# Transposed inputs laid out by the host, and a reordered preparation, in a two-layer cross attention

## What is computed

```
q = heads(x @ w_q);  k, v = heads(text @ w_k), heads(text @ w_v)
out = softmax(q k^T / sqrt(8)) v  +  softmax(masked or normed token scores) v_ip
x = out @ w_out + b_out + x
```

## Time and profile before

| | |
|---|---|
| median of 3 runs | 1545.47 us (1544.97 to 1546.61) |
| the profiled execution | 1546.61 us, its span 1544.8 us |
| TensorE, VectorE, ScalarE busy | 94%, 72%, 69% of the span |
| queries' block / prepare / attention starts | 0 to 38.7 / 38.7 to 200.7 / 200.7 us |

### The profile page before, as it was taken

The page is one execution under the profiler, slowest core; times in us unless marked ns, Lnnn a source line. Parts: engine busy times, 40 slices in busy tenths (PEclk is TensorE's granted clock), DMA queues, the critical chain, the costliest instruction groups (busy, mean ns, idle before and its releaser), DMA issues. The chain is left out here.

```text
span 1544.8 us, 32772 instructions
## 1 busy us (share of the span) xinstructions
PE 1456.3 (94%) x12886; PEld 911.6 (59%) x12886; DVE 1119.0 (72%) x1572; ACT 1061.7 (69%) x1962; POOL 189.6 (12%) x363
## 2 busy tenths in 40 slices
PE   6899969999999999899999999999999999999995
PEld 4455513333333333577777777777777777777774
DVE  5777778887877877876767777777777777777625
ACT  2455548877877877777777777777777777777752
POOL 4553300000101101000010000000000000000000
PEclk9899969999999999999999999999999999999996
DMA  5256741111211211100001100000011000100000
GB/s 158 67 168 196 223 101 51 51 51 51 56 47 50 64 47 47 42 23 24 20 22 34 28 20 23 26 24 23 19 26 26 23 18 25 26 23 16 7 1 18
DMA packets 82903, 75.91 MB, mean 49 GB/s; under 512 B 28608, under 2 KB 70964, under 8 KB 82756
## 3 DMA queue, kind: packets, MB, share of 16 engines
q1 hardware_dynamic: 82756, 73.88, 17.7%
HBM read 47.73 MB, written 26.09 MB: 48 GB/s over the span
## 5 line engine op out<-in xcount | busy, mean ns | idle before, releaser
L1367 DVE TENSOR_TENSOR whole<-late,whole 128x1024 f16<-128x1024 f32 (+1 forms) x280 | 320.2, 1144 | 99.7 <-ACT whole L1226 96.5
L1352 DVE TENSOR_REDUCE mx<-ps_y 128x2 f32<-128x800 f32 (+2 forms) x227 | 224.0, 987 | 106.1 <-PE ps_y L1034 105.9
L1112 PE MATMUL ps_v<-eh,whole 128*128 128x269 f16 x1040 | 292.7, 281 | 0.0
L1112 PE MATMUL ps_n<-eh,whole 128*128 128x269 f16 x1040 | 291.4, 280 | 0.0
L1226 ACT CAST whole<-late 128x1024 f16<-128x1024 f32 (+1 forms) x280 | 275.8, 985 | 8.9
L1114 PE MATMUL ps_v<-el,whole 128*128 128x269 f16 x960 | 268.9, 280 | 0.0
L1115 PE MATMUL ps_v<-eh,whole 128*128 128x269 f16 x960 | 268.8, 280 | 0.0
L1115 PE MATMUL ps_n<-eh,whole 128*128 128x269 f16 x960 | 268.1, 279 | 0.0
L1114 PE MATMUL ps_n<-el,whole 128*128 128x269 f16 x960 | 267.9, 279 | 0.0
L1352 DVE TENSOR_REDUCE mx<-ps_x 128x2 f32<-128x800 f32 (+2 forms) x198 | 195.5, 987 | 80.9 <-PE ps_x L1034 80.7
L1352 DVE TENSOR_REDUCE mx<-ps_t 128x2 f32<-128x800 f32 (+2 forms) x215 | 211.5, 984 | 32.8 <-PE ps_t L1034 32.5
(11 more groups left out here) (433 smaller groups left out, 2073.6 us busy)
## 6 DMA issues: line engine op xcount, KB each, us to landing
e<-in_ctx SPq DMA_DIRECT2D x4, 1536.0 KB
kb<-k_parts SPq DMA_DIRECT2D x80, 74.9 KB
kb<-k_parts SPq DMA_DIRECT2D x80, 74.7 KB
k_parts<-kp SPq DMA_DIRECT2D x12, 400.0 KB
vb<-v_cols SPq DMA_DIRECT2D x40, 117.0 KB, 2.0
v_cols<-late SPq DMA_DIRECT2D x4, 1040.0 KB, 10.8
late<-v_cols SPq DMA_DIRECT2D x40, 104.0 KB, 2.0
qb<-q_parts SPq DMA_DIRECT2D x160, 25.0 KB
```

Of the source, the lines that this page charges most:

```text
L1112: pe.matmul(ps, hi, eh, start=(t == 0), stop=False)
L1352: nc.vector.tensor_reduce(mx[:, pair % 2, c, :], bank("max", pair, c)[:, :, 0:w], AX.X, ALU.max).then_inc(chunk_max, 1)
L1367: nc.vector.tensor_tensor(pl[s % 2][:, t0:t0 + w, :], ring[:, turn % EXPS, 0:w], ph[s % 2][:, t0:t0 + w, :], ALU.subtract).then_inc(low_do ...
```

## The change

The host gives three more inputs: x, the context and the tokens, each transposed. The transposes and their copies in `queries` and `prepare` go. `ctxT` is loaded by DMA in four pieces for each batch (`load_piece`), a piece of the next batch when the value products no longer read its columns. The keys are sent segment by segment, each with a semaphore of its own (`k_sent[m]`); segment 0 goes out before SP waits for `el_done`. The next batch's maximum is taken behind the ninth value tile of this one, and its all-reduce follows the last third part. The second parts are cast by ScalarE. In batch 0, `scale_bits`, `high` and `low` come behind all ten key products, GpSimd's all-reduces come before its clearing, and the softmax steps move behind the values of batches 0 and 1. All loops are written out. Pairs 0 and 1 are loaded in batches 2 and 3, pairs 2 and 3 at the start of the attention. The queries' large buffers lie in `eh`. The lines of the diff that matter:

```diff
+            ctx = (ctx_in, sbuf("e32", [P, NT, C], F32, st), sbuf("ctxT", [P, 2, NPAD], F32, st),
+                   st.enter_context(nc.semaphore("ctx_loaded")), [st.enter_context(nc.semaphore(f"turned_in_{kc}")) for kc in range(4)])
+            w_ctx = (sbuf("wk", [P, 2, 2 * D], F32, st), sbuf("wv", [P, 2, 2 * D + IP[1]], F32, st), st.enter_context(nc.semaphore("weights_in")))
+            queries(nc, K, LS, banks, w, consts, QS, ctx, w_ctx, (x, bbox, spatial))
+            prepare(nc, K, L, banks, ctx, w_ctx, consts, KS, QS, VS)
...
+                def send_keys(b, m):
+                    if m < 2:
+                        sp.wait_ge(k2_done, KI * b + 4 * (m + 1))
+                        for seg, r0, rows, l, h0 in KSEG:
+                            if seg == m:
+                                for part in range(3):
+                                    dst = KS[l][h0:h0 + rows // DH, b, part]
+                                    sp.dma_start(dst, kp[r0:r0 + rows, m, part, :]).then_inc(k_sent[m], 16)
+                        return
+                    sp.wait_ge(k2_done, KI * (b + 1))
+                    for j in range(2):
+                        for part in range(3):
+                            dst = KS[1][H - KREST // DH:H, b, part].rearrange("h d (g j k) -> h d g j k", j=2, k=KC)[:, :, :, j]
+                            src = kp[KREST * j:KREST * (j + 1), 2, part, 0:2 * KC].rearrange("p (g k) -> p g k", k=KC)
+                            sp.dma_start(dst, src).then_inc(k_sent[2], 16)
+
+                def load_turned(b, kc):
+                    n = KI + min((kc + 1) * KC - 1, TOK - 1) // P
+                    if kc == 3:
+                        n = LASTF
+                    sp.wait_ge(filled[n % 8], fills(b - 1, n))
+                    load_piece(sp, consts, ctxT, turned_in, b, kc)
+
+                def send_values(b, half):
+                    t0, t1 = ((0, NT // 2), (NT // 2, NT))[half]
+                    sp.wait_ge(vh_done, NT * b + t1)
+                    sp.dma_start(VS[0][:, b, :, t0:t1].rearrange("g p t n -> p g (t n)"),
+                                 vaug[:, :, t0:t1].rearrange("p g t i n -> p g (t i n)")).then_inc(v_sent, 16)
+
+                for b in range(B):
+                    send_keys(b, 0)
+                    if b < B - 1:
+                        sp.wait_ge(el_done, 2 * (b + 1))
+                        sp.dma_start(e32[:, 0:NT - 1, :], ctx_in[b + 1, 0:P * (NT - 1)].rearrange("(t p) c -> p t c", p=P)).then_inc(ctx_loaded, 16)
+                        sp.dma_start(e32[0:LAST, NT - 1, :], ctx_in[b + 1, P * (NT - 1):TOK]).then_inc(ctx_loaded, 16)
+                    send_keys(b, 1)
...
+                        load_pair(sp, K, KS, QS, b - 2)
+                    if b < B - 1:
+                        load_turned(b + 1, 0)
+                        load_turned(b + 1, 1)
+                        send_values(b, 0)
+                        load_turned(b + 1, 2)
+                        load_turned(b + 1, 3)
+                        send_values(b, 1)
+                        sp.wait_ge(freed[LASTF % 8], fills(b, LASTF))
+                        send_cut_v(sp, K, VS, L, b)
+                sp.wait_ge(v_sent, 16 * 2 * (B - 1))
+                load_v0(sp, K, VS, 0)
+                for m in range(3):
+                    sp.wait_ge(k_sent[m], 16 * SENDS[m] * B)
...
-                turn(1)
-                with sp.Fori(2, B, 1) as b:
-                    turn(b)
-                send(B - 1)
-                sp.wait_ge(k_sent, 16 * SENDS * B)
...
-                    pe.wait_ge(ctx_loaded, 32 * (b + 1))
-                    for n in range(TR):
-                        ps = bank(n)
-                        for t in range(2 * n, min(2 * n + 2, NT)):
-                            for c in range(2):
-                                at = ((t % 2) * 2 + c) * P
-                                last = pe.transpose(ps[:, at:at + P], e32[:, t, c * P:(c + 1) * P], K["ident"][:])
-                        last.then_inc(filled[n % 8], 1)
...
+                            pe.wait_ge(turned_in[kc], 16 * (b + 1))
...
+                def second_part(b, n):
+                    m, kc = n // 4, n % 4
+                    act.wait_ge(freed[n % 8], fills(b, n))
+                    nc.scalar.copy(kp[:, m, 1, kc * KC:(kc + 1) * KC], rem[:, n % RR, :]).then_inc(k1_done, 1)
...
+                for b in range(B):
+                    for n in range(KI):
+                        m, kc = n // 4, n % 4
+                        if kc == 0 and b:
+                            act.wait_ge(k_sent[m], 16 * SENDS[m] * b)
+                        act.wait_ge(filled[n % 8], fills(b, n))
+                        nc.scalar.copy(kp[:, m, 0, kc * KC:(kc + 1) * KC], banks[n % 8][:, 0:KC]).then_inc(k0_done, 1)
+                        if n:
+                            second_part(b, n - 1)
+                        if b and n == 3:
+                            high(b)
+                    second_part(b, KI - 1)
+                    if not b:
+                        high(b)
+                    if b == 1:
...
+                def over_partitions(column, b):
+                    pool.wait_ge(amax_done, b + 1)
+                    nc.gpsimd.partition_all_reduce(amax[:, column + 1:column + 2], amax[:, column:column + 1], P,
+                                                   bass.bass_isa.ReduceOp.max).then_inc(amax_all, 1)
+
+                over_partitions(2, 0)
+                over_partitions(0, 1)
                 nc.gpsimd.memset(vaug, 0.0)
                 nc.gpsimd.memset(vcut, 0.0).then_inc(pool_init, 1)
...
+                    if b < B - 1:
+                        over_partitions(0, b + 2)
...
+                def largest(b):
+                    dve.wait_ge(ctx_loaded, 32 * (b + 1))
                     nc.vector.tensor_reduce(amax[:, 0:1], e32[:], AX.XY, ALU.max, apply_absolute_value=True).then_inc(amax_done, 1)
+
...
+                dve.wait_ge(weights_in, 64)
+                nc.vector.tensor_reduce(amax[:, 2:3], wv[:, :, D:2 * D], AX.XY, ALU.max, apply_absolute_value=True).then_inc(amax_done, 1)
+                largest(0)
+                nc.vector.memset(K["eh"][:, :, NT - 1, :], 0.0).then_inc(init, 2)
+                nc.vector.memset(K["el"][:, :, NT - 1, :], 0.0).then_inc(init, 1)
+                nc.vector.memset(expo[:, 0:1], 118.0).then_inc(init, 1)
+                nc.vector.tensor_copy(K["identb"][:], K["ident"][:]).then_inc(init, 1)
+                dve.wait_ge(init, 5)
+                for b in range(B):
...
+                        nc.vector.tensor_tensor(rem[:, n % RR, :], banks[n % 8][:, 0:KC], kp[:, m, 0, kc * KC:(kc + 1) * KC],
+                                                ALU.subtract).then_inc(freed[n % 8], 1)
+                        if b and n == 1:
+                            scale_bits(b)
+                        if b and n in (5, 6):
+                            low(b, n - 5)
+                    if not b:
+                        scale_bits(b)
+                        low(b, 0)
+                        low(b, 1)
...
+                        if t == 8 and b < B - 1:
+                            largest(b + 1)
+                    if b == 0:
+                        centre(nc.vector, link, L, 0, L["mask"], smax).then_inc(centred, 1)
+                    if b == 1:
+                        dve.wait_ge(exp_done, 1)
+                        link(normalise(nc.vector, link, L, 0, None, ssum))
...
+def load_piece(sp, consts, ctxT, turned_in, b, kc):
+
+    k0, k1 = 400 * kc, 400 * (kc + 1) if kc < 3 else TOK
+    sp.dma_start(ctxT[:, :, k0:k1], consts["ctxT"][b, :, k0:k1].rearrange("(c p) k -> p c k", p=P)).then_inc(turned_in[kc], 16)
...
+                load(xT0, consts["xT"][0:P], x_in)
+                load(xT1[0:R1], consts["xT"][P:D], x_in)
                 load(w0[:], wq[0:P], w_in)
                 load(w1[0:R1], wq[P:D], w_in)
-                for b in range(B):
-                    load(tokens[b * IP[0]:(b + 1) * IP[0], :], ctx_in[b, TOK - IP[0]:TOK, :], first_in)
+                load(K["ipT"][:].rearrange("p c b n -> p c (b n)"), consts["tokT"].rearrange("(c p) n -> p c n", p=P), tok_in)
...
+                for kc in range(4):
+                    load_piece(sp, consts, ctxT, turned_in, 0, kc)
+                load(e32[:, 0:NT - 1, :], ctx_in[0, 0:P * (NT - 1)].rearrange("(t p) c -> p t c", p=P), ctx_loaded)
+                sp.wait_ge(zeroed, 1)
+                load(e32[0:TOK - P * (NT - 1), NT - 1, :], ctx_in[0, P * (NT - 1):TOK, :], ctx_loaded)
+                for h in range(2):
+                    load(K["xq"][:, h * NH * 2:(h + 1) * NH * 2], x[2 * h:2 * h + 2].rearrange("b (h p) c -> p (b h) c", p=P), first_in)
+                load(K["ident"][:], consts["ident"], first_in)
                 load(boxes[:].rearrange("p b m c -> p (b m c)"), bbox.rearrange("b m c -> (b m c)").partition_broadcast(P), boxes_in)
...
+                vaug = LS[0]["vaug"]
```

(35 more changed lines are left out.)

311 lines of the change are left out of this document (81 added, 230 removed).

## The result

The changed kernel took 1555.67 us in the median of five runs (1554.87 to 1561.41), the kernel before 1546.61 (1544.97 to 1549.07) beside it: a ratio of 1.0065, 95% interval 1.0049 to 1.0081. It is slower by 0.65%, some 10 us. The profiled executions differ by 9.1 us in their spans (1553.9 and 1544.8).

The account below looks back on a forecast made before the run. No engine was full in the preparation; a ring of hand-overs around a buffer's reload and the key sends set each batch. Terms -4.2 + 7.2 + 2.8 + 2.4 - 5.9 = +2.3 us on 1545.47 gave 1548, range 1531 to 1558.

Parts of the forecast that it names:

- Queries, -4.2: Queries' block: loads landing some 5.3 us earlier, less 1.1 us for a collision; -4.2 us, bounds -5.3 and -2.7.
- The collision: Queries: late `xq` puts GpSimd's addition beside VectorE's last cut; cost taken as 1.1 us, bounds 0 and 2.6.
- First batch, +7.2: Preparation to the fifth key product of batch 1: 62.2 us of the block instead of 55.0, +7.2 us.
- the 1.4 for `scale_bits`: Batch 0: `scale_bits` behind all ten key products takes 1.4 us, ahead of `high`, `low` and the reload.
- The pieces: Context loads: first lands 19.0 us behind the reload's issue, fourth 24.8; then the third key product takes 1.4.
- the periods of +2.8 and +2.4: Batches 1 and 2, between fifth key products: 38.1 us against 35.3, and 39.6 against 37.2.
- The rival of a queue that drains at its best rate: Key sends and pieces: 12.5 us instead of 19.0 in three places, -19.5 us, time 1528; chance 0.18.
- Last batch, -5.9: Last preparation batch, without reload or pieces: 28.6 us against 34.5 to the attention, -5.9 us.
- the first rival: The DMA queue drains at 353 GB/s in the preparation: -19.5 us, time 1528; chance 0.18.
- The clearing during GpSimd's code change: Batch 0: GpSimd's clearing overlaps its code change, the reload's buffer free 6.7 us earlier, time 1541; chance 0.10.
- Everything on the ring (1557): Preparation: slow fourth part beside `low`, segment 0 out with the reload, half-clock products; 3.1 us or more three times; chance 0.22.
- The attention, 0: Attention: loading pairs 2 and 3 there costs nothing, covered by the maxima of pairs 0 and 1.

Follow-up runs that it names:

- x2: Changed kernel with the loads of `xq` and of the identity moved ahead of the context pieces; 1557.1 us, ratio 1.0066 to the kernel before.
- x1: Changed kernel with GpSimd's clearing of `kb` held until VectorE has written both low parts of the first batch; 1551.9 us, ratio 1.0034 to the kernel before.
- x9: Changed kernel with each of two `kb` clearings cut into four short ones at the same place; 1553.6 us, ratio 1.0056 to the kernel before.
- x7: Changed kernel without loaded pieces, all batches using batch 0's context (a bound), first subtractions awaiting all earlier third parts; 1538.3 us, ratio 0.9949.
- x4: Changed kernel: batch 0's keys ahead of the reload, later batches' first two pieces ahead of segment 2, first subtractions awaiting all earlier third parts; 1556.0 us, ratio 1.0061.
- x6: x5 with VectorE's `centre` ahead of the maximum of batch 1 instead of behind it; 1542.0 us, ratio 0.9979 to the kernel before.
- x8: x5 with `centre` and `normalise` moved behind the fourth subtraction of batches 1 and 2; 1542.5 us, ratio 0.9974 to the kernel before.
- x12: x11 with `centre` and `normalise` moved behind the fourth subtraction of batches 1 and 2; 1535.7 us, ratio 0.9936 to the kernel before.
- x10: Changed kernel with VectorE's next-batch maximum taken late again, at the head of that batch; 1556.7 us, ratio 1.0068 to the kernel before.
- x5: Changed kernel joining x1, x2 and x4's order, but with all four pieces ahead of segment 2's sends; 1541.1 us, ratio 0.9960 to the kernel before.
- x11: x5 with x9's short clearings of `kb` in place of x1's wait; 1539.5 us, ratio 0.9953 to the kernel before.

## Why the prediction came out as it did

- *Queries, -4.2, measured +1.2.* The list of loads did land earlier (L727 at 16.18 instead of 19.57, 3.4 us; 5.3 predicted). TensorE had waited 1.8 us for it, then ran its value products in part at 1.2 GHz (granted clock 0.50 from 19.0 to 22.3, where two rows took 1.99 and 1.92 us instead of 1.37), and the way to the second cut took 12.3 us instead of 10.7. The collision was taken at 1.1 "since they meet only in part": they met in full, 2.8 us (x2); the upper bound of 2.6 was near it. So nearly all of the miss of 5.4 us is three terms of like size: the list 1.9, the way to the cut 1.6, which the prediction put at nothing, and the collision 1.7.
- *First batch, +7.2, measured +12.5.* The step that failed is "`scale_bits`, `high` and `low` stand behind all ten in batch 0: 1.4, 3.0, 4.1 and 0.7". The order of the edges was right and the tenth subtraction ended near the time given (25.5 us into the block, 26.8 predicted). What failed is the 1.4 for `scale_bits`: it took 8.9, since it was priced as if nothing of GpSimd lay beside it. Third parts made it 3.4 (x1), the clearing 8.9. The prediction followed GpSimd's list to the third parts and not one instruction further, to the clearing of `kb` that comes next (x1, x9). The same lock was priced for the queries in the paragraph before.
- *The pieces* (19.0, 24.8, 1.4): 18.4 and 26.2 together, right, and the periods of +2.8 and +2.4 with them (+3.6, +2.9). The working is less exact than its result: 21.1 less 3.1 plus 1.2 is 19.2 and not 19.0, and the fifth product followed the first piece by 7.8 us because two products ran at half clock, not because the fourth piece was the last wait. The two paths ended within 1 us of each other. x7 shows that the pieces are the loss: 17 us. The rival of a queue that drains at its best rate (12.5 us) is refuted.
- *Last batch, -5.9*: -6.7.
- *The range.* 1531 is not half of the first rival, as the prediction says: half of -19.5 us would be 1538.
- *Rivals.* The clearing during GpSimd's code change: its first third part came 19.5 us into the block (20.2 predicted), so no. Everything on the ring (1557) comes nearest in time, but its condition did not hold: the fourth part took 0.95 us (it was the fifth that met `low`, 4.06 us), and segment 0 went out 5.2 us before the reload. Its half clock at the first products was real.
- *The attention, 0, measured -4.4.* Here the prediction said that it would be wrong if more than 1 us moved. The two misses and the three small ones add up to +11.2 us, and this took 4.4 of them back: that the time lies inside the range is luck. See below.

## What to carry to other kernels

When a step is moved, look at what the other engine of the pair VectorE and GpSimd does at its new place, to the end of that instruction: nine tiny operations took 8.9 us instead of 1.4, most of it beside one long clearing. When compute is replaced by loads, put each load on the queue at the place where its consumer needs it: here the pieces cost 17 us, and another order gave back some 12 of the 20 us by which they delayed the attention. And when a wait is taken away, list what is next; x4, x6 and x8 each only moved one, and x12 gained because the next two went together.

## What the runs showed of the hardware

- GpSimd idles before some kinds of instructions: 6.8 us and more from an all-reduce to the third parts (8.7 in x10's first), 6.5 to 7.0 from clearings to the third parts, and 6.1, 6.6 and 8.9 from clearings to an all-reduce (x1, x5, x8), most of these rows with nothing that it waits for ("issue"); before its first all-reduce it is 5.4. In x6 (8.2) the input of the all-reduce stood ready only 1.0 us before it. Clearings behind an all-reduce or a third part start at once (45.96 and 68.43 in after). The Trainium skill ("GPSIMD Engine Reference", section "Instruction dispatch") has about 6 us for the first call of newly loaded code; our rows, from 5.4 to 8.9 us, are mostly somewhat longer, and no run here shows that loading is what they are.
- The attention and close, whose code is the same in all the kernels but for SP's first loads, took 1339.7 to 1344.2 us. Compared pair by pair, after gains 0.5 us on before in the first 40 us, 0.8 more up to the change of layer and 3.0 in the close. The granted clock goes along with it in part: it is 0.50 for 27.3 us at the start and 19.4 in the close, 30.7 and 25.2 before. x4, with 30.7 and 20.6 us, takes 1343.4; x9 and x11, with 27.3 and 25.6, take 1341.8; x2, with 27.3 and 24.3, takes 1344.0. What decides the length of these stretches stays open; a gain of up to 4 us in the preparation can vanish in them, as in x2, or appear, as in after.
